# Expert up product with its operands swapped: weights stationary, turned tokens moving

## The reference

```
x2   = layernorm(x)                       # 1250 x 768
gate = x2 @ Wg + bg                       # 8 experts
scores, idx = top_k(gate, 2)
h_e  = gelu(x2 @ W1[e] + b1[e])           # 768 -> 384, exact GELU
y_e  = h_e @ W2[e] + b2[e]                # 384 -> 768
out  = x + sum over the 2 chosen experts of score * y_e
```

## Time and profile before

| | |
|---|---|
| median of 3 runs | 1097.65 us (1095.04 to 1099.85) |
| span of the profiled execution | 1093.1 us |
| median of the runs less that span | 4.55 us |
| mean granted TensorE clock | 0.944 |
| TensorE busy | 960.1 us (88%), 6377 matmuls |
| TensorE weight loads | 696.5 us (64%) |
| VectorE busy | 786.1 us (72%) |
| ScalarE busy | 333.6 us (31%) |
| GpSimd busy | 134.9 us (12%) |

### The profile page before, as it was taken

One profiled execution on the slowest core, in us unless ns is written; L12 is line 12 of the kernel. 1 busy time (PEld: TensorE's weight loads), 2 busy tenths in 40 slices (PEclk: granted clock), 3 DMA queues, 4 the chain that ended last, 5 costly groups with the idle time before them and its releaser, 6 DMA issues.

```text
span 1093.1 us, 17219 instructions
## 1 busy us (share of the span) xinstructions
PE 960.1 (88%) x6377; PEld 696.5 (64%) x6379; DVE 786.1 (72%) x1757; ACT 333.6 (31%) x402; POOL 134.9 (12%) x139
## 2 busy tenths in 40 slices
PE   3699999998979989989979889977888659999994
PEld 2667767775544446445759889956885536666662
DVE  6576789778884687897578977869988944444442
ACT  3561122112004422431323332314434622222220
POOL 3010000000001000000000000000421034555541
PEclk9899999999989999999989999977998769999998
DMA  7340221225251728538669010004217656878771
GB/s 227 125 157 21 68 73 58 73 77 230 102 189 45 241 88 275 170 98 264 225 232 426 30 49 1 1 1 176 85 32 273 254 201 164 195 188 190 189 163 20
DMA packets 62091, 155.05 MB, mean 142 GB/s; under 512 B 12708, under 2 KB 32038, under 8 KB 59066
## 3 DMA queue, kind: packets, MB, share of 16 engines
q1 hardware_dynamic: 49226, 111.94, 29.4%
q0 software_dynamic: 9936, 34.23, 12.7%
q10 hardware_dynamic: 2848, 7.77, 1.8%
HBM read 107.95 MB, written 48.94 MB: 144 GB/s over the span
## 4 chain that ended last, share of the span: by engine, by line
PE 66%; DVE 22%; issue 4%; DMA 4%; ACT 2%; SPq 1%; DVEq 0%; POOLq 0%; ACTq 0%
PE PS L1753 39%; PE PS L2002 12%; DVE arena L1452 3%; PE PS L1829 3%; DVE arena L1458 3%; DVE arena L1496 3%; PE PS L2153 2%; PE PS L1840 1%; PE PS L1809 1%; PE PS L1844 1%; DVE arena L1468 1%; DMA arena<-in_L_gnn_W_dram 1%; DVE arena L1358 1%; DVE arena L1208 1%; DMA arena<-as_d 1%
## 5 line engine op out<-in xcount | busy, mean ns | idle before, releaser
L1753 PE MATMUL PS<-arena 128*128 128x384 f16 (+7 forms) x3396 | 564.0, 322 | 5.7 <-DVE arena L1743 3.0
L1753 PEld LDWEIGHTS PS<-arena 128*128 128x128 f16 (+2 forms) x3396 | 320.7, 99 | 215.3 <-issue 13.3
L2002 PE MATMUL PS<-arena 128*128 128x193 f32 (+1 forms) x1200 | 191.3, 323 | 21.7 <-DVE arena L1458 16.3
L2002 PEld LDWEIGHTS PS<-arena 128*128 128x128 f32 x1200 | 186.7, 200 | 26.3 <-DVE arena L1458 16.0
L1018 ACT ACTIVATE arena<-arena,AS 128x1280 f32<-128x1280 f32 x60 | 81.9, 1365 | 133.9 <-DVE arena L1452 133.7
L1452 DVE SCALAR_TENSOR_TENSOR arena<-arena,AS 128x1280 f32<-128x1280 f32 x60 | 94.5, 1578 | 0.0
L1458 DVE SCALAR_TENSOR_TENSOR arena<-arena 128x1280 f32<-128x1280 f32 x60 | 90.9, 1514 | 2.5 <-PE PS L2002 2.4
L1260 DVE TENSOR_SCALAR arena<-arena 128x240 f16<-128x240 f16 x324 | 90.5, 279 | 0.0
L1259 DVE TENSOR_SCALAR arena<-arena 128x128 f16<-128x128 f16 x324 | 81.4, 251 | 0.1
L1742 DVE SCALAR_TENSOR_TENSOR arena<-PS,arena 128x768 f32<-128x768 f32 x27 | 25.9, 958 | 62.6 <-PE PS L1753 58.0
L1095 ACT ACTIVATE arena<-PS 128x1536 f16<-128x1536 f16 x27 | 39.2, 1451 | 75.7 <-PE PS L2153 75.7
(11 more groups left out here) (265 smaller groups left out, 966.8 us busy)
## 6 DMA issues: line engine op xcount, KB each, us to landing
arena<-in_L_ffn_W_dram SPq DMA_DIRECT2D x48, 384.0 KB, 4.0
fr_d<-arena SPq DMA_DIRECT2D x48, 384.0 KB, 3.2
arena<-fr_d SPq DMA_DIRECT2D x16, 1152.0 KB, 14.6
arena<-in_x_dram SPq DMA_DIRECT2D x18, 384.0 KB, 5.2
arena<-rr_d SPq DMA_DIRECT2D x4, 1280.0 KB, 8.4
g_d<-arena SPq DMA_DIRECT2D x10, 388.0 KB, 2.3
acc_d<-arena SPq DMA_DIRECT2D x10, 384.0 KB, 2.6
xf_d<-arena ACTq DMA_DIRECT2D x10, 384.0 KB, 3.0
```

Source lines behind the costliest of these rows:

```text
L1753: m = T.matmul(out, left[i][x], right[i][y], start=first and i + r == 0, stop=last and 3 * i + r == n - 1)
L2002: m = T.matmul(ps[b][:, r * (C + 1):(r + 1) * (C + 1)], PT[i % deep][:, d * P:(d + 1) * P], feats, start=t == 0 and r == 0, stop=t == NT - ...
```

## The change

The operands of `up` change sides. For each of the three blocks of 128 inner columns, the expert's weights are stationary and the turned rows move (128 columns): 3 x 18 = 54 matmuls. The result comes out turned, an inner column per partition, so `turn` and its semaphore go. The inner bias is then one word per partition: VectorE picks it per tile into `fb1t` ahead of the loop, from `fb1c`, the experts' biases loaded as columns (three copies by the sync queue), and ScalarE adds it inside GELU, which reads PSUM in three pieces. `inner` goes, and `split` reads `Hb` in SBUF. The gathered bias row shrinks to `b2`. On TensorE the order becomes: number, `rows_in(i+1)`, `up(i)`, `down(i-1)`; on VectorE `split(i+1)`, then the sum of tile `i`.

```diff
-        BW = HID + D
-        BR = v3(reg(O_X, BB * BW), BB)
-        Hp = low(5 * D, HID)
+        BR = v3(reg(O_X, BB * D), BB)
+        fb1c = small(HC * NE).rearrange("p (m e) -> p m e", m=HC)
+        fb1t = small(HC * NTL).rearrange("p (m i) -> p m i", m=HC)
+        fb1p = big(3 * HID, HC * NTL * NE).rearrange("p (m i e) -> p m i e", m=HC, i=NTL)
...
-            sp.dma_start(fb_d[:, 0:HID], fb1).then_inc(s_row_in, 16)
-            sp.dma_start(fb_d[:, HID:BW], fb2).then_inc(s_row_in, 16)
+            sp.dma_start(fb_d, fb2).then_inc(s_row_in, 16)
...
             for u in freed:
                 experts(u)
+            with nc.allow_non_contiguous_dma("bias columns"):
+                for m in range(HC):
+                    sp.dma_start(fb1c[:, m, :], fb1[:, m * P:(m + 1) * P].rearrange("e p -> p e")).then_inc(s_row_in, 16)
             sp.wait_ge(s_fin_psum, NT)
...
             def gelu(i):
-                act.wait_ge(s_hp_ready, i + 1)
+                act.wait_ge(s_h_psum, i + 1)
+                act.wait_ge(s_fb1_ready, 1)
                 if i:
-                    act.wait_ge(s_ht_psum, i)
-                a.activation(Hb, Hp, ACT.Gelu).then_inc(s_h_ready, 1)
+                    act.wait_ge(s_ht_ready, i)
+                for m in range(HC):
+                    k = a.activation(Hb[:, m * P:(m + 1) * P], ps[2 + i % 2][:, m * P:(m + 1) * P], ACT.Gelu, bias=fb1t[:, m, i:i + 1], scale=1 / UP)
+                k.then_inc(s_h_ready, 1)
...
+            dve.wait_ge(s_row_in, 16 * 9)
+            link(V.tensor_tensor(ct, eid.rearrange("p (i a) -> p i a", a=1).to_broadcast([P, NTL, NE]), seq8.to_broadcast([P, NTL, NE]), ALU.is_equal))
+            for m in range(HC):
+                i = V.tensor_tensor(fb1p[:, m], ct, fb1c[:, m:m + 1, :].to_broadcast([P, NTL, NE]), ALU.mult)
+            link(i)
+            V.tensor_reduce(fb1t.rearrange("p m i -> p (m i)"), fb1p.rearrange("p m i e -> p (m i) e"), axis=AX.X, op=ALU.add).then_inc(s_fb1_ready, 1)
             dve.wait_ge(s_map_psum, 2)
...
-            def inner(i):
-                dve.wait_ge(brows_in[i % 2], 16 * (i // 2 + 1))
-                dve.wait_ge(s_h_psum, i + 1)
-                if i:
-                    dve.wait_ge(s_h_ready, i)
-                V.scalar_tensor_tensor(Hp, ps[2 + i % 2][:, 0:HID], 1 / UP, BR[:, i % BB, 0:HID], ALU.mult, ALU.add).then_inc(s_hp_ready, 1)
...
-                link(V.tensor_copy(ht[:, 0], ps[4][:, 0:HID]))
-                V.tensor_tensor(ht[:, 1], ps[4][:, 0:HID], ht[:, 0], ALU.subtract).then_inc(s_ht_ready, 1)
-
-            inner(0)
+                link(V.tensor_copy(ht[:, 0], Hb))
+                V.tensor_tensor(ht[:, 1], Hb, ht[:, 0], ALU.subtract).then_inc(s_ht_ready, 1)
+
+            split(0)
             for i in range(NTL):
                 if i < NTL - 1:
-                    split(i)
-                    inner(i + 1)
-                if i == NTL - 2:
-                    split(NTL - 1)
+                    split(i + 1)
                 yb = Yb[:, i % 2, :]
+                dve.wait_ge(brows_in[i % 2], 16 * (i // 2 + 1))
                 dve.wait_ge(s_y_psum, i + 1)
...
             def up(i, e):
                 pe.wait_ge(s_xrt_ready, i + 1)
                 if i >= 2:
-                    pe.wait_ge(s_hp_ready, i - 1)
-                product(ps[2 + i % 2][:, 0:HID], [(XRTP[:, i % 2, 0, k, :], XRTP[:, i % 2, 1, k, :]) for k in range(KC)],
-                        [[FR[:, 0, bass.ds(e, 1), r, k * HID:(k + 1) * HID] for r in (HI, LO)] for k in range(KC)]).then_inc(s_h_psum, 1)
-
-            def turn(i):
-                pe.wait_ge(s_h_ready, i + 1)
-                if i:
-                    pe.wait_ge(s_ht_ready, i)
-                for k in range(HC):
-                    m = T.transpose(ps[4][:, k * P:(k + 1) * P], Hb[:, k * P:(k + 1) * P], ident[:, :])
-                m.then_inc(s_ht_psum, 1)
+                    pe.wait_ge(s_h_ready, i - 1)
+                for m in range(HC):
+                    u = product(ps[2 + i % 2][:, m * P:(m + 1) * P], [[FR[:, 0, bass.ds(e, 1), r, k * HID + m * P:k * HID + (m + 1) * P] for r in (HI, LO)] for k in range(KC)],
+                                [(XRTP[:, i % 2, 0, k, :], XRTP[:, i % 2, 1, k, :]) for k in range(KC)])
+                u.then_inc(s_h_psum, 1)
...
-                if i:
-                    turn(i - 1)
                 up(i, e)
                 if i:
                     down(i - 1, before)
                 before = e
-            turn(NTL - 1)
             down(NTL - 1, before)
```

More of the change, by code:

```diff
@@ L240, in gps_layer @@
         assert NS * P // 2 + NQ * NS * NTL // 2 <= 6 * D
-        BW = HID + D
         BB = 4
-        BR = v3(reg(O_X, BB * BW), BB)
-        assert BB * BW <= 6 * D
-        Hp = low(5 * D, HID)
+        BR = v3(reg(O_X, BB * D), BB)
         TE = NT * NE
@@ L289, in gps_layer @@
         onesh = small(1).bitcast(F16)
+        fb1c = small(HC * NE).rearrange("p (m e) -> p m e", m=HC)
+        fb1t = small(HC * NTL).rearrange("p (m i) -> p m i", m=HC)
+        fb1p = big(3 * HID, HC * NTL * NE).rearrange("p (m i e) -> p m i e", m=HC, i=NTL)
+        assert HC * NTL * NE <= 2 * D
         xf_d = nc.dram_tensor("xf_d", (NP + P, D), F32, kind="Internal").ap()
         acc_d = nc.dram_tensor("acc_d", (NP, D), F32, kind="Internal").ap()
-        fb_d = nc.dram_tensor("fb_d", (NE, HID + D), F32, kind="Internal").ap()
+        fb_d = nc.dram_tensor("fb_d", (NE, D), F32, kind="Internal").ap()
         bias_d = nc.dram_tensor("bias_d", (D,), F32, kind="Internal").ap()
@@ L476, in gps_layer @@
         s_brow1_in = sem("brow1_in")
-        s_hp_ready = sem("hp_ready")
+        s_fb1_ready = sem("fb1_ready")
         s_nt_psum = sem("nt_psum")
@@ L499, in gps_layer @@
         s_h_ready = sem("h_ready")
-        s_ht_psum = sem("ht_psum")
         s_ht_ready = sem("ht_ready")
@@ L854, in _ @@
             pool.wait_ge(s_slots_ready, 1)
-            pool.wait_ge(s_row_in, 16 * 7)
+            pool.wait_ge(s_row_in, 16 * 9)
             pool.wait_ge(s_map_psum, 2)
@@ L1713, in _ @@
             link(V.tensor_scalar(score[:, 1, :], score[:, 0, :], 128.0, None, ALU.mult))
-            def inner(i):
-                dve.wait_ge(brows_in[i % 2], 16 * (i // 2 + 1))
-                dve.wait_ge(s_h_psum, i + 1)
-                if i:
-                    dve.wait_ge(s_h_ready, i)
-                V.scalar_tensor_tensor(Hp, ps[2 + i % 2][:, 0:HID], 1 / UP, BR[:, i % BB, 0:HID], ALU.mult, ALU.add).then_inc(s_hp_ready, 1)
             Y = PS[:, 5 * 512:7 * 512].rearrange("p (a n) -> p a n", a=2)[:, :, 0:HALF]
             def split(i):
-                dve.wait_ge(s_ht_psum, i + 1)
+                dve.wait_ge(s_h_ready, i + 1)
                 if i >= 2:
@@ L1741, in _ @@
                     dve.wait_ge(sums_out[i % 2], 16 * (i // 2))
-                link(V.scalar_tensor_tensor(yb.rearrange("p (a n) -> p a n", a=2), Y, 1 / UP, BR[:, i % BB, HID:BW].rearrange("p (a n) -> p a n", a=2), ALU.mult, ALU.add))
+                link(V.scalar_tensor_tensor(yb.rearrange("p (a n) -> p a n", a=2), Y, 1 / UP, BR[:, i % BB, :].rearrange("p (a n) -> p a n", a=2), ALU.mult, ALU.add))
                 V.tensor_scalar(yb, yb, score[:, 1, i:i + 1], None, ALU.mult).then_inc(s_y_ready, 1)
```

## The result

| | before | after |
|---|---|---|
| median of 4 runs | 1097.22 us (1095.04 to 1099.85) | 1114.73 us (1112.19 to 1115.82) |
| ratio to before | | 1.0153, 95% interval 1.0129 to 1.0178 |
| span of the profiled execution | 1093.1 us | 1113.1 us |
| mean granted TensorE clock | 0.944 | 0.942 |
| start of the first rows' transposes, tile 0 | 886.03 us | 889.22 us |

A forecast was written before the change was run, and what follows sets the result against it. TensorE was taken as the bound: its array before, its instruction queue after the change. 23 x 0.50 = +11.5, start -0.9, tail +1.3 and -1.6 gave +10.3 us, so 1107.9 us; range 1094 to 1130.

The forecast's parts named there:

- The step that set the sign: Steady loop: the larger of queue's 7.35 us and array's 6.62 us sets the period, +0.50 us per tile.
- the queue's turn: TensorE's instruction queue, per tile: addresses, number read, transposes and waits add up to 7.35 us.
- Rival 1: Steady loop: the queue doesn't bind, the array's 6.62 us holds; 11.2 us faster, 1086.4 us; chance 0.13.
- rival 4: Whole loop: pieces of the queue's turn overlap, period 7.0 us, total change within 5.5 us; chance 0.10.
- Rivals 2 and 3: `up` on the array: pairs take 0.083 us, 1126 us, chance 0.07; register-addressed weight loads slow, 1166 us, chance 0.06.
- The price of an address: TensorE's queue: each block under a dynamic address takes 0.127 us, so 36 in `up` take 4.57 us.
- the forecast's upper bound: Queue's turn: if handing over the transposes costs the 0.8 us between the waits, the period is 7.85 us.
- "Can a lead hide it?": Start of `up`: the queue is about 1 us ahead, gone by two thirds of `up`, so addresses aren't hidden.
- Start: Loop's first tiles: GELU needs no gather and `up(1)` follows `up(0)` at the queue's pace, -0.9 us.
- End: Loop's last tiles: +1.3 us to the end of `down(25)`, -1.6 us in the wait before `down(26)`.
- Costs put at nothing: GELU pieces and split hide under `down`; VectorE's work, about 2.6 us, and bias copies ahead of the loop cost nothing.
- One sign was announced wrongly: Within `up`: TensorE would show idle for "issue", with matmul starts about 0.085 us apart.

The follow-up runs named there:

- e1: The changed kernel with `up` always using expert 0's weights at fixed addresses, 12 addresses per tile: 1091.59 us, ratio 0.9952.
- e2: The kernel before, operands not swapped and `turn` kept, with `up` in three blocks of 128 columns: 1117.39 us, ratio 1.0204.
- e11: The changed kernel in order `up` blocks 0 and 1, `down` half 0, block 2, half 1, number read per tile: 1109.54 us, ratio 1.0094.
- e8: The changed kernel with `down` using expert 0's weights at fixed addresses, `up` keeping its 36: 1110.03 us, ratio 1.0108.
- e3: The changed kernel with all 27 expert numbers loaded into registers once ahead of the loop: 1114.55 us, ratio 1.0170.
- e10: The kernel before with `up` using expert 0's weights at fixed addresses, 12 addresses per tile: 1097.51 us, ratio 1.0006.
- e6: The changed kernel with single `up` blocks and `down` halves alternating, and expert numbers read ahead of the loop: 1117.13 us, ratio 1.0186.
- e7: The kernel before with only `turn(0)` moved after `up(1)` and `turn(26)` between the halves of `down(25)`: 1095.70 us, ratio 1.0001.
- e5: The changed kernel with single `up` blocks and `down` halves alternating, number read per tile: 1129.77 us, ratio 1.0296.
- e9: The changed kernel, numbers read ahead, in order `up` blocks 0 and 1, `down` half 0, block 2, half 1: 1097.31 us, ratio 0.9999.

## Why the prediction was right, and where its size was off

**The step that set the sign held.** +10.3 us were forecast and +17.5 measured. The forecast put the period at the queue's turn, not at the array's, and named 48 addresses per tile. The queue's rows of after show 48; without 36 of them the period falls to the array's 6.61 (e1; forecast 6.62); with them and without the swap it is there all the same (e2). No other engine or transfer comes into it: the pieces of the chain between the transposes are matmuls of line 1755 and no releaser is named. Rival 1 wanted 6.62 us and rival 4 a change within 5.5 us; neither came. Rivals 2 and 3 fell with e1 and e2.

**The term that was mis-sized is the queue's turn: 7.35 forecast, 7.596 measured.** +0.246 over 23 tiles is 5.7 of the 6.8 us that were missing. I averaged the distances between the starts of the queue's operations over some 19 tiles of after:

| part of the turn | forecast | measured |
|---|---|---|
| 48 addresses | 48 x 0.127 = 6.10 | 48 x 0.132 = 6.34 |
| the number, from its load to the next wait | 0.65 | 0.82 |
| three waits and twelve transposes | 0.30 + 0.30 | 0.43 |
| sum | 7.35 | 7.59 |

The price of an address was read from 11 gaps between rounded starts. Most gaps are 0.124 us, but every eighth or so has some 0.05 more, and 48 times 0.005 is 0.24. The load of the number took 0.30 us in the loop of before and longer in that of after:

```profile
L2186 PEldq TENSOR_LOAD <-arena x23: 300/489/709, 911.6 to 1078.8; - x23
```

A duration read from one kernel didn't hold in the other. In e11 the median is 0.317, and there the period is 7.475: 0.09 of the 0.12 us between the two orders is the slower load. The transposes cost the queue almost nothing, less than the 0.30 assumed, so the 0.8 us that stood between the waits in before, the forecast's upper bound, can't have been their price. It was the full queue that the forecast called probable: at the wait behind it 17 matmuls had not begun, in before as in e8.

**"Can a lead hide it?"** The answer, no, was right, and the lead at the start of `up` is the 1 us forecast (the address at 950.9, the matmuls in the chain from 952.07). The forecast let the queue run ahead as far as it liked. In after this made no error, since the queue was 13 to 16 matmuls ahead at that wait and never stopped; it made the expectation of e3 wrong by 0.5 us per tile.

**Start**: -1.03 us against -0.9 forecast (17.43 to 16.40). From the first address to the transposes of tile 3 the sum gave 13.4 us and the trace has 13.4 (892.2 to 905.62), at a granted clock of 1.00 where before had 0.88, though with 0.56 us of idle array for "issue" ahead of `up(1)`, where the forecast had none. The side of before is less firm: e10, with the same order and as many matmuls of the same shapes, had a start of 15.63 us in its profiled execution, 1.8 less, so the size of the gain rests on which execution was profiled.

**End**: +0.8 us against -0.3. The timeline:

```profile
1080.32 0.83 PE L2155 MATMUL PS<-identh,arena 128*128 128x128 f16 x12
1080.99 14.43 PE L1755 MATMUL PS<-arena 128*128 128x128 f16 x144
1097.38 4.78 PE L1755 MATMUL PS<-arena 128*128 x18 [1.96 <-DVE arena L1745]
```

To the end of `down(25)` it is 15.1 us, where 14.3 was forecast: the same addresses, load and waits, longer than in the sum once more. The wait behind it is 1.96 us for 1.83, and the last products take 4.78 us for 4.59.

**Costs put at nothing** were nothing as far as the profile can say. GELU in three pieces, 0.88 us, and the split, 0.95, end about 1.9 us after `up` (at most 2.5 forecast), under the 3.1 us of `down`; e6 shows what it costs without that cover.

```profile
955.88 0.88 ACT L1093 ACTIVATE arena<-PS,arena 128x128 f32<-128x128 f32 x3 [2.32 <-PE PS L1755]
956.79 0.36 DVE L1732 CAST arena<-arena 128x384 f16<-128x384 f32 x1 [3.68 <-ACT arena L1093]
957.18 0.56 DVE L1733 TENSOR_TENSOR arena<-arena 128x384 f16<-128x384 f32 x1
```

The loop began 3.2 us later than before (889.22 for 886.03). That isn't the copies of the biases or the added work of VectorE. The same operation of ScalarE in the attention, a stage that the change doesn't touch, in before and in after:

```profile
L1018 ACT ACTIVATE arena<-arena,AS x60: 1362/1365/1370, 564.1 to 813.0; 128x1280 f32<-128x1280 f32 x60
L1020 ACT ACTIVATE arena<-arena,AS x60: 1361/1362/1367, 567.4 to 816.3; 128x1280 f32<-128x1280 f32 x60
```

At 567 us after is 3.3 us behind already; the sync queue issues the copies at 830 us, and VectorE's products run from 888.3. From the first of these operations to the loop it is 321.9 us in before and 321.8 in after: the work ahead of the loop cost nothing, as forecast. Single executions differ by as much without the change: e2's loop began at 884.3 us, e7's at 889.2 and e10's at 891.5. The profiled execution of before was among its shortest (1.6 us lie between span and median in after, 4.1 in before), which about cancels these 3.2.

Together: 5.7 for the period, 1.1 for the end and -0.1 for the start make 6.7 of the 6.8 us between 1107.9 and 1114.73. (The other 0.4 us between +10.3 and +17.5 is the median of before, 1097.65 in three runs and 1097.22 in four.)

**One sign was announced wrongly.** The prediction wanted to see TensorE idle for "issue" within `up`. Next to none is recorded (0.3 us put down to "issue", 1.04 us idle in all, of the 174.70 of the steady part), since the matmuls' recorded durations cover the gaps. The starts 0.085 apart are there, but only where the lead is gone, from the middle of `up` on (the prediction said by two thirds); over all 54 of the tile shown it is 0.070.

## What to carry to other kernels

Where operands have addresses that depend on data, count the distinct blocks per stage and set them against the array's time for the stage: 0.13 us per block here, so a block whose matmuls take the array less than that makes the queue the bound, however busy the array looks. Cut such operands as wide as the instruction takes, or spread the narrow ones between work that needs few addresses; a surplus that comes all at once can't be stored, because the queue got only 17 matmuls ahead. To see whether the array is fed, compare the distances between starts with the same shape elsewhere, not its busy time.

## What the runs showed of the hardware that was not expected

- The queue's lead has an end at 17 matmuls with their loads (e8, e3, e1 and before, at the wait behind the transposes). In time that is 1.6 us with 5 long ones among them, 0.95 us with short ones alone.
- A load of one word into a register took 0.30, 0.32, 0.49 or 1.03 us at the median, by the order of the work around it (before, e11, after, e5). The reason is open.
- At the loop's start the array had gaps that no wait explains. The second turn of e1:

```profile
897.89 1.57 PE L1755 MATMUL PS<-arena 128*128 128x128 f16 x20
899.75 0.34 PE L1755 MATMUL PS<-arena 128*128 128x128 f16 x3 [0.29 <-issue]
900.48 0.44 PE L1755 MATMUL PS<-arena 128*128 128x128 f16 x5 [0.40 <-issue]
901.26 0.39 PE L1755 MATMUL PS<-arena 128*128 128x128 f16 x4 [0.34 <-issue]
902.00 0.44 PE L1755 MATMUL PS<-arena 128*128 128x128 f16 x5 [0.35 <-issue]
903.46 5.49 PE L1755 MATMUL PS<-arena 128*128 128x128 f16 x35 [1.02 <-issue]
```

Three to five matmuls, then a gap, every 0.75 us, while the DMA engines were 85 to 92% busy with the first gathers. The same pattern, in part, stands in e3, e6, e8 and e9, whose starts took 19.3 to 21.7 us, and not in after (16.4) or before. It could be instructions that arrive late behind the gathers; that is a guess, and no run tested it.
